# A decoder layer on one core: the prologue of the pipeline rewritten, and keys and queries loaded by three transfers a group

## The reference

```python
x = _layernorm(x + _L0_attn_ref(x, ...))                 # 16 heads, key width 8, value width 16
x = _layernorm(x + _L0_xattn_ref(x, ctx_1024, ...))      # 16 heads of 16, softmax over 512 keys
x = _layernorm(x + _L0_ffn_ref(x, ...))                  # sigmoid(xr W_r) * (relu(xk W_k)^2 W_v)

# in _L0_attn_ref
log_gate = jax.nn.log_sigmoid(kg) / GATE_NORM
def step(state, inp):
    state = state * gg[..., None] + kk[..., :, None] * vv[..., None, :]
    out = jnp.einsum('bhd,bhde->bhe', qq, state)
...
o = (o - mu) * lax.rsqrt(var + EPS)
return gate * o @ Wo                                     # gate = silu(inputs @ Wg + bg)

# in _L0_xattn_ref
scores = jnp.einsum('bqhd,bkhd->bhqk', Q, K) / jnp.sqrt(jnp.float32(HEAD_DIM))
attn = jax.nn.softmax(scores, axis=-1)
```

## Time and profile before

| | us |
|---|---|
| median of 3 runs (577.40, 578.76, 581.91) | 578.76 |
| the profiled execution: its own time | 579.01 |
| its span in the trace | 576.6 |
| PE, DVE, ACT, POOL busy | 474.7, 398.2, 291.6, 219.4 |
| first score tile of step 0 (the prologue's end for PE) | 113.58 |

### The profile page before, as it was taken

How to read it: one execution, slowest core, us unless ns; L and a number is a source line. 1 busy time by engine, 2 the same in 40 slices (tenths; PEclk the granted TensorE clock), 3 DMA queues, 4 the chain that set the end, 5 groups by cost and what they waited for, 6 DMA issues and landing times. The chain is left out here.

```text
span 576.6 us, 6249 instructions
## 1 busy us (share of the span) xinstructions
PE 474.7 (82%) x1925; PEld 200.1 (35%) x1925; DVE 398.2 (69%) x641; ACT 291.6 (51%) x509; POOL 219.4 (38%) x210
## 2 busy tenths in 40 slices
PE   8999356697987768989889869797988878798885
PEld 3433221142431213354333314453422333243454
DVE  5899968835678597537797896569647757732285
ACT  2146320145476383724758755436776523677434
POOL 6566666533067586231558783223000001000000
PEclk9999875588997899989989999989989978898898
DMA  7476324111278511111765203120311110000011
GB/s 228 159 191 178 106 86 136 36 36 37 83 194 200 110 55 57 56 37 64 184 155 128 57 3 90 55 66 1 106 46 42 57 36 3 1 1 1 1 36 36
DMA packets 35295, 45.48 MB, mean 79 GB/s; under 512 B 5920, under 2 KB 29120, under 8 KB 35264
## 3 DMA queue, kind: packets, MB, share of 16 engines
q1 hardware_dynamic: 32144, 38.02, 23.0%
q10 hardware_dynamic: 3120, 7.08, 4.9%
HBM read 34.93 MB, written 9.96 MB: 78 GB/s over the span
## 5 line engine op out<-in xcount | busy, mean ns | idle before, releaser
L1396 DVE TENSOR_REDUCE MX<-bank 128x1 f32<-128x512 f32 x256 | 166.8, 681 | 123.4 <-PE bank L574 120.8
L1046 ACT ACTIVATE PT<-bank 128x512 f32<-128x512 f32 x256 | 146.7, 598 | 138.8 <-PE bank L583 131.3
L574 PE MATMUL bank<-KS,QS 96*128 96x512 bf16 x232 | 91.5, 399 | 37.4 <-DVE MX L1396 27.3
L583 PE MATMUL bank<-QS,KS 99*128 99x512 bf16 x256 | 100.8, 405 | 14.8 <-ACT PT L1046 14.3
L1712 POOL TENSOR_TENSOR W<-qT,W 128x512 f32<-128x512 f32 x48 | 61.8, 1289 | 40.6 <-DVE W L1315 26.6
L597 PE MATMUL bank<-PT,Vs 128*32 128x512 f32 x512 | 74.4, 655 | 1.8 <-ACT PT L1046 0.8
L583 PEld LDWEIGHTS bank<-QS,KS 99*128 99x128 bf16 x256 | 24.4, 99 | 102.8 <-issue 52.4
L574 PEld LDWEIGHTS bank<-KS,QS 96*128 96x128 bf16 x232 | 22.9, 99 | 94.3 <-DVE MX L1396 59.7
L1698 POOL TENSOR_TENSOR W<-kT,W 128x512 f32<-128x512 f32 x32 | 46.3, 1450 | 6.6 <-ACT kT L904 6.6
L1743 POOL TENSOR_TENSOR MP<-MX,zero 128x16 bf16<-128x16 f32 x15 | 4.9, 324 | 101.9 <-issue 52.7
L1536 DVE TENSOR_TENSOR_SCAN W<-bank,W 128x512 f32<-128x512 f32 x32 | 38.8, 1218 | 2.5 <-DVE W L1521 0.2
(11 more groups left out here) (213 smaller groups left out, 729.6 us busy)
## 6 DMA issues: line engine op xcount, KB each, us to landing
W<-v_rows SPq DMA_DIRECT2D x12, 512.0 KB, 6.4
W<-v_rows ACTq DMA_DIRECT2D x12, 512.0 KB, 6.3
KS<-k_parts SPq DMA_DIRECT2D x96, 64.0 KB, 2.3
...
```

Source lines behind the costliest of these rows:

```text
L574: pe.matmul(bank(n)[:, :], QS[0:NS, h, i * P:(i + 1) * P], KS[0:NS, h, :], start=True, stop=True).then_inc(filled(n), 1)
L583: pe.matmul(bank(name)[:, :], KS[0:NR, h, kt * P:(kt + 1) * P], QS[0:NR, h, :], start=True, stop=True).then_inc(filled(name), 1)
L1046: act.activation(PT[:, n % 2, j, :], bank(name)[:, :], ACT.Exp).then_inc(emptied(name), 1)
L1396: dve.tensor_reduce(MX[:, NT * h + i:NT * h + i + 1], bank(n)[:, :], AX.X, ALU.max).then_inc(emptied(n), 1)
```

## The change

It does six things.

1. `pick` is made by ACT and no longer by DVE.
2. Sequence 0: DVE issues product e + 1 before scan e. All second products go to POOL (`OWN_PRODUCTS` is gone), the first of them after its 13th multiplication.
3. PSUM rests in place: gate, variance, the sums `o0` and `o1` and the remainders of keys and queries are worked on in the bank they were computed in, by ACT and DVE, and not copied to `ab`, `oS` and `full32` first. K0, K1 and the gate of sequence 1 stand elsewhere in PE's list, and matmuls without a use (`keep_busy`) lie in four gaps and among the maxima.
4. The first layer norm is done by ACT (scale and bias), not DVE.
5. The maxima of heads 0 to 3 come in one piece; scans 11 to 15 of sequence 1 stand behind them, and the eight tiles of heads 4 and 5 go into the slots of step 0 (its own row of `MAXIMA`). The second row of maxima (`mr1`) uses bank 0 and stands a quarter later.
6. In every step: `k_parts` and `q_parts` are laid out by feature and head. A group is loaded by three transfers: parts 0 to 2 at slot 0, parts 0 and 1 at slot 3, part 0 at slot 5 for keys; for queries part 0 three times, part 1 twice, part 2 once, the copies made by a source dimension of step 0. The parts go out by two transfers (m) where one did it.

```diff
-SLOTS_K = [0, 0, 1, 1, 0, 2]
-SLOTS_Q = [0, 1, 0, 1, 2, 0]
+SLOTS_K = [(0, 3), (3, 2), (5, 1)]
+SLOTS_Q = [(0, 0, 3), (3, 1, 2), (5, 2, 1)]
...
-    *((f"m{h}.{i}", 0, 3 + i % 2) for h in range(4, LAG) for i in range(NT)),
...
-OWN_PRODUCTS = [0, 7, 11, 15]
+EARLY_SCANS = 11
+MAXIMA[0] = {**dealt("b", 0, (5, 7, 8, 7, 6, 3, 5, 2, 3, 2), range(4, H)), **NEXT_MAXIMA}
...
-ROWS = {(2, 3): ("b", 1), (5, 3): ("b", 2), (10, 3): ("b", 3), (15, 0): ("o", 0)}
+ROWS = {(3, 0): ("b", 1), (5, 3): ("b", 2), (10, 3): ("b", 3), (15, 0): ("o", 0)}
...
+            def keys_of(b, g, at, parts_in):
+                src = t["k_parts"][b, 0:parts_in, :, 4 * g:4 * g + 4, :].rearrange("p d h n -> p d (h n)")
+                sp.dma_start(KS[HD * at:HD * (at + parts_in), 4 * g:4 * g + 4, :], src).then_inc(K_in[g], 16)
+            def queries_of(b, g, at, part, times):
+                src = t["q_parts"][b, part, :, 4 * g:4 * g + 4, :].rearrange("d h n -> d (h n)")
+                sp.dma_start(QS[HD * at:HD * (at + times), 4 * g:4 * g + 4, :],
+                             src.unsqueeze(0).broadcast_to([times, HD, 4 * S])).then_inc(Q_in[g], 16)
+            def part_out(dram, b, p, m, done):
+                dst = t[dram][b, p].rearrange("d (m h) n -> m h d n", m=ND)[m]
+                sp.dma_start(dst, parts[:, p, m, :]).then_inc(done, 16)
...
+                sp.wait_ge(Q_out0[0], 16)
+                queries_of(0, 0, *SLOTS_Q[0])
+                sp.wait_ge(*read("Q0", 0))
+                part_out("q_parts", 0, 2, 0, Q_out0[2])
...
                 by_feature("K0", 0, xwk, 0, cT)
-                by_feature("K1", 0, xwk, 1, cT)
...
+                keep_busy("gy0", 0, 4)
                 pe.wait_ge(gated0, 2)
                 by_token("gy0", 0, oS, wo, 0)
                 by_token("gy1", 0, oS, wo, 1)
-                pe.wait_ge(x1_done, count(NT, 0, NT))
+                by_feature("K1", 0, xwk, 1, cT)
+                keep_busy("gt0", 0, 12)
+                pe.wait_ge(x1_0, NT)
...
+                keep_busy("s0.0", 0, 8)
+                for h in range(4):
                     for i in range(NT):
                         first_max(h, i)
+                        keep_busy("s0.0", 0, 1)
+                    if h == 1:
+                        reduce_four(1, 1)
+                keep_busy("s0.0", 0, 6)
                 max_rows(0, 0)
+                keep_busy("s0.0", 0, 8)
                 reduce_four(1, 2)
-                for h in range(4, LAG):
-                    for i in range(NT):
-                        first_max(h, i)
...
+                act.wait_ge(nb_set, 1)
+                for tt in range(NT):
+                    act.activation(x1b[:, 0, tt, :], xtok[:, tt, :], ACT.Identity, bias=nb[:, tt:tt + 1],
+                                   scale=rs[0][:, tt:tt + 1]).then_inc(x1_0, 1)
...
             def scale_half(m):
-                dve.wait_ge(o_gate0, m + 1)
-                dve.tensor_tensor(oS[:, m, :], oS[:, m, :], rsd, ALU.mult).then_inc(gated0, 1)
+                dve.tensor_tensor(oS[:, m, :], bank("var", 0)[:, :], oS[:, m, :], ALU.mult).then_inc(gated0, 1)
...
+                first_product(0)
                 for e in range(DV):
-                    first_product(e)
+                    if e + 1 < DV:
+                        first_product(e + 1)
                     first_scan(0, e)
...
-                for e in (8, 9):
+                for e in range(9, EARLY_SCANS):
                     first_scan(1, e)
                 for h in range(4):
                     for i in range(NT):
                         max_tile(0, h, i)
-                    if h < 3:
-                        first_scan(1, 10 + h)
                 first_parts()
-                first_scan(1, 13)
+                for e in range(EARLY_SCANS, DV):
+                    first_scan(1, e)
                 gate_log(1)
-                first_scan(1, 14)
...
                 for e in range(DV):
+                    if e == 13:
+                        second_product(0)
                     multiply(0, e)
```

394 lines of the change are left out of this document (196 added, 198 removed), and 12 rows, old and new, of the table PROLOGUE.

## The result

The changed kernel is **no faster, and slightly slower**: 582.39 us (median of 20 runs, 577.55 to 587.61) against 578.86 for the kernel before (20 runs beside it, 572.99 to 583.86); ratio 1.008, 95% interval 1.0053 to 1.0107. That is 3.5 us or 0.8%: clear of noise over 20 runs, but inside the 1% that I had taken for no change. I had said 562, range 553 to 573. The profiled execution took 579.93 us with a span of 578.1 (before: 579.01 and 576.6).

A forecast was written before the change was run, and what follows sets the result against it. The time before step 0 was taken as one chain of dependent steps, with PE not at its limit. 579.0 less 21.2 up to the first score plus 4.0 in steps 0 to 3 gave 561.8, so 562 us; range 553 to 573.

The forecast's parts named there:

- part 4: From the turn to the first maximum: it comes at 76.8 us, total gain 11.0, so this part gains almost nothing.
- part 5: From the first maximum to the first score: parts at 87.9, first score at 92.4 us, total gain 21.2.
- the slow rival: Engines serve query groups 0 and 1 mixed, steps 0 to 2 wait 31 us in all: 589 us, chance 0.04.
- the query loads bind: Group 0's 32 packets take 8.6 us in every step, adding 3.1, 3 and 4: 572 us, chance 0.12.
- the two rivals: Deferred work (clock 0.5, 60 to 100 us): 570 us, 0.16; late queries (slot 10 waits over 5 us): 572, 0.12.
- Part 1: Up to the last product of sequence 0: POOL ends it at 46.4 us, a gain of 1.8.
- Part 2: From there to the gated output: ready at 53.3 us, total gain 7.0, bounds 5 and 8.
- Part 3: From the gated output to the first norm: the turn moves from 71.97 to 61.4 us, total gain 10.6.
- Eight tiles: Tiles of heads 4 and 5 moved into step 0: 0.22 us each on PE plus waits for two banks, +2.5 us.
- The moved row `mr1`: In the steps, the second row of maxima in bank 0 saves 0.7 us.
- The logarithm: The gate's logarithm behind five scans on DVE delays ACT's first exponential to 9.5 us after the parts: +0.5 us.
- spread copies: Copies spread over all sixteen engines, so the 2.1 and 4.0 us of load losses go: 555 us, chance 0.08.

The follow-up runs named there:

- rows16_steps: rows16, but the first sequence's loads keep the changed kernel's copy-by-copy row order (3 and 2 engines): median 565.75 us, ratio to before 0.985.
- rows16: The changed kernel with copied query rows and key rows laid feature by feature, so copies use sixteen engines: median 558.94 us, ratio to before 0.965.
- changed_mr1_back: The changed kernel with the second row of maxima again in slot 2, quarter 3, and bank 3: median 589.94 us, ratio to before 1.0238.
- rows16_tiles_back: rows16 with the eight tiles of heads 4 and 5 ahead of step 0 again: median 555.06 us, ratio to before 0.9663.
- rows16_log_first: rows16 with DVE doing the second gate's logarithm after one of the five late scans, not all: median 555.54 us, ratio to before 0.9666.
- rows16_no_fill: rows16 without the filling matmuls of no use ahead of step 0: median 557.08 us, ratio to before 0.9706.

## Why the prediction was wrong

**The step that failed is the query loads**, in part 4, in part 5 (where they hold up the row of maxima) and in the steps. I saw the mechanism before the run (three and two engines, and the packet count now shows them) and mis-sized it: 2.1 us ahead of the first maximum and 4.0 in the steps, where undoing it gave back 7.5 and 14.1 (spans of rows16_steps against rows16 and the changed kernel). That loads in copies run on so few engines was an inference from the packets of `mrow` and the key slots, loads without copies; the shares of 0.19 and 0.12 and the 432 packets bear it out. I used it for a price of packets on the loads alone. Three things were missing from that price.

- *What stands behind the copies.* My sum ended at the first maximum. The transfer of `mrow` has three closing packets itself and a share of 0.21 while it runs alone, about three engines too, and its last packet ended 8.2 us after its issue and not 1.8, behind groups 2 and 3. That made 5.74 us of idle PE ahead of the first score. Part 5 counted the row's own way at 3.3 us from the earlier trace rows, rows in which no copies were under way.
- *The clock.* The 5.74 us took the full clock of slot 0 with them (0.50 in its projection, 1.00 in rows16), which I had booked at -2.3, and the wait at slot 10 of step 1 cost more than itself (3.09 us of idle, slot longer by 4.9).
- *When group 0 lands, and when PE wants it.* For engines that carry nothing but the copies the packet price was right: from 188 to 193 us 4 KB packets went at 18 a microsecond (90 of them, 0.16 us each: three engines), and then at about 12 (two engines; share 0.12 from 195 to 197). PE went on at 193.67, and 62 such packets followed in the 5 us after 193. So group 0 was served ahead of group 1, and the slow rival (both mixed, step 0 waiting until 202) did not happen. In steps 1 and 2 I allowed 0.3 and 0.7 us; the waits were 3.09 and 3.06. In step 1 the last closing packet before PE went on came at 314.16, 12.2 us after the first load was asked for, where I had counted 10.2: from 306 to 311 us all sixteen engines were full (share 1.01), with 243 packets of ACT's queue beside 72 of SP's, and a packet of 4 KB took about 0.29 us. PE also stood ready 1.8 us earlier than before (311.28 for 313.10), since slots 2 to 4 had become shorter. In step 2 the loads were asked for at 416.81, 2.1 us later than before, of which 0.8 was the step's own delay: the last outgoing part had been issued by 413.82 and not 412.43, and from there to the first load it took 3.0 us and not 2.3. The second issue of each outgoing part, which I had put into SP's idle time at nothing, is in that.

The rival "the query loads bind" added 10.1 to my 4.0 for the steps, and 14.1 is what undoing them gave back. That agreement is luck: it rested on 0.27 us a packet in every step, and the 14.1 hold slower clocks and a later issue as well. It missed `mrow`, the tiles and the rest ahead of step 0, and therefore ended at 572. Of the signs I had named, closing packets of 3 and 2 came; the clock was not at 0.5 from 60 to 100 us (1.00, 0.97, 0.69 and 1.00 in windows of 10 us), and no wait at slot 10 of steps 1 and 2 exceeded 5 us, so neither of the two rivals showed as I had said it would, and the forecast was wrong all the same.

**Part by part**, against the changed kernel, with rows16 for what the loads hide:

- Part 1 was right: POOL's last product of sequence 0 ended at 46.31 (42.58 + 3.73; 46.4 foreseen), and DVE's first product started at 14.02 (14.9 foreseen; a gain of 1.5, just over my bound of 1.3, and without effect on POOL's end). The cast that stayed on DVE took 5.08 us beside POOL's memset, nearly what the copy had taken (5.56); it ended at 12.74, the memset at 12.66. Part 2 too: 53.84 for 53.3, after 60.31. Part 3: 62.69 for 61.4.
- Part 4: 82.43 for 76.8. Without the slow loads 79.29, where my sum without them gives 74.7. Of the 4.6 left the turn has 1.9. SP has 1.1: its six key loads took 3.75 us to issue, so the first outgoing query part, ready at 67.9, was issued 2.3 later, at 70.22, and I had allowed 1.2. The other 1.6 I did not trace.
- Part 5: my 103.07 for the end of the last four maxima should read 102.97 (100.31 + 2.66), which changes nothing. The maxima took 13.6 us in rows16, not 11.1, for PE stood at half clock at the start (granted 0.50 from 79.3 to 83 us, a maximum every 0.85 us) and a sum of POOL's products stands among them. From the parts to the score 3.5 in rows16 (4.5 foreseen), 9.3 in the changed kernel. First score in sum: 12.4 us late, of which rows16 gives back 8.4.
- Eight tiles: 2.5 foreseen, 6.6 measured. I priced them by PE's 0.22 us, and what PE waits for there is DVE's reduction, 0.68 each (8 x 0.68 is 5.4).
- The moved row `mr1`: -0.7 foreseen, about 8 measured. I took the shorter way of the row and not the wait for bank 3 with the low clock behind it, which stood in the profile of before (3.05, 2.03, 2.03 and 0.89 us ahead of this transpose in the four steps; granted 0.57, 0.63 and 0.63 in the 4 us behind the first three). This error went the other way and hid part of the loads' cost: with the move undone the change is 2.4% slower than before (changed_mr1_back). That the result lies as near to 562 as it does is owed to it.
- The logarithm (+0.5): in rows16 the first exponential came 8.2 us after the parts (9.5 foreseen), 4.7 behind the first score. Making it early moved slot 1 by 0.1 us beyond what was there before, so it cost the step nothing. Right in the sum.
- The sum itself: my working for step 1 has group 0 landing at 312.8, ahead of its use at 313.10, and books 0.3 as a loss. It is small beside the error above.

For rows16 the sum comes close, by errors of both signs. It has 96.42 for the first score, 6.1 over my 90.3 without slow loads, and 460.1 us from there to the end, 2.9 under the 463.0 of before (I had 0.0 without loads): together 3.2 over the 553.3 us that my milestones give without slow loads. The rival "spread copies" said 555, and rows16 measured 558.94. For the changed kernel, 12.4 us more than foreseen stand ahead of the first score and 6.2 behind it. Of the 6.2, slot 10 has +7.1 (11.1 for 4.0), the tiles +4.4 and slot 0 +1.8; what is left, about -7, is the row `mr1` beyond my 0.7, and agrees with the 8 that undoing it showed. It is a remainder, not a measurement of its own.

What stays open: why slot 10 of step 0 waits 2.86 us even in rows16, and where rows16_tiles_back found 4 us in step 3 (its granted clock was 1.00 from 470 to 520 us, that of rows16 0.78 to 0.88 in four of the five windows there; one execution each). Slot 10 of step 0 lasted 9.6 to 9.9 us in rows16_log_first, rows16_no_fill and rows16_steps and 11.9 in rows16, which is open too.
